# Moving the chain that makes dt ahead in four engines' orders, and one of its additions from GpSimd to VectorE

## The chip, the cores and the metric

The kernel runs on one core of a Trainium2 chip. The metric is the device time of one execution in microseconds, the median of several executions. Engine names are those of the profile: PE is TensorE, DVE is VectorE, ACT is ScalarE, POOL is GpSimd, and SP is the engine whose queue issues nearly all DMAs. A core's engines run their own instruction lists in order and meet only through semaphores.

## The reference

A decoder block over x of shape (4, 512, 512): first a Mamba layer with an MLP on the layer-normed input, then a quantized attention-like product, then a feed-forward layer with 4-bit weights. The change touches only the Mamba part, which is, cut to what matters:

```
zxbcdt = x @ in_proj_w.T                        # z, x, B, C and dt_in
dt  = softplus(dt_in @ dt_proj_w.T + dt_proj_b) # 1024 channels, 512 tokens
dA  = exp(dt[..., None] * A)                    # 16 states per channel
dBx = (dt * x) (x) B
h_i = dA_i * h_(i-1) + dBx_i                    # the recurrence over the tokens
y   = sum over the states of C_i * h_i, + D_skip * x
out = (y * silu(z)) @ out_proj_w.T
```

For large negative arguments the logarithm in softplus loses digits. The kernel computes softplus(v) = max(v, 0) + log(1 + e) + ((1 - (1 + e)) + e) with e = exp(-|v|); the last bracket is what 1 + e lost by rounding. The first half of the bracket, 1 - (1 + e), is made by ACT in two instructions into `sp_abs`; the addition of e is the one that the change moves.

## The kernel before, in words

The first stage, up to about 1034 us of 2797, is the scan. It runs over 32 steps (`g`): 4 batches times 8 tiles of 128 channels. Each step has 16 units (`c`), one for each state, each a tile of 128 partitions by 512 tokens. Per unit:

- PE spreads one row group of v = dt * x over the partitions (`spread_v`, from the tile `vpack`) and one of dt (`spread_dt`, from `dpack`), both with the selection matrix `sel` (both are L1806);
- ACT makes the decay exp(dt * A) in place in PSUM (`decay`, L896);
- DVE multiplies v by B (`make_drive`, L1392, tile `drive`) and runs the recurrence (`scan`, L1401, tile `state`). DVE's list is drive of the next unit, scan of this unit, and so on;
- POOL multiplies the state by C (`read_out`, L1233, tile `read`), and PE sums four of these at a time into y (`gather_four`, L1822, and L1820 for the skip term at the first four).

The scan of unit n waits for its decay; `spread_dt` of unit n+3 waits for the scan of unit n, as three PSUM banks are in turn. `read_out` uses a ring of 8 tiles, so its unit n waits until the gather of unit n-8 is done, and `state` is a ring of 6.

Beside this, step g makes what step g+1 and g+2 need, as lines spread over the units:

- in units 0 to 11 PE makes three tiles (jobs) of the input projection (L1757 to L1759, tiles `whi`, `wlo`), which ACT takes to SBUF (`take`, L830) and SP stores to DRAM (`spill`, L536) and later reads again. Step g with (g + 2) mod 8 = 7 has no jobs. The tiles of x and B of a new batch come in steps 6, 14 and 22, and each goes out in four scattered copies, `x_d<-ev` and `b_d<-ev`;
- the softplus for step g+2: PE makes the product (`dt_project`, unit 11), ACT then runs `soft_abs`, `soft_pos`, `soft_exp`, `soft_one` (two instructions) and `soft_log` at units 12 to 15;
- the rest of dt for step g+1: POOL runs `soft_rest` (the moved addition, tile `sp_rest`, L1182), `soft_sum` (L1188), `soft_dt` (L1197, tile `dt_t`) and `dt_x` (L1205, tile `v_t`) after the read_out of units 0, 1, 2, 3. ACT rounds dt and v to the PE's format (`dt_high` L872 at unit 6, `v_high` L876 at unit 8), POOL makes the remainders (`dt_low` L1210 at unit 7, `v_low` L1215 at unit 9), and SP copies all four, in halves, to `dpack` and `vpack` (`load_pack_dt`, `load_pack_v`, L554 to L558);
- a few things more on POOL: `normalise` in steps 2 and 4 (four each), `out_weights_low` in steps 29 and 30 (L1221, two each).

All orders are written out by hand in the loops below. SP's list in a step is: load of B, weights and spill for the first job, load of C, store of y, weights for the second, dt and v packs, spill of the second job, load of x for g+2, weights and spill of the third. SP waits in that order, so a wait holds up all behind it.

After the scan come the output projection, the two MLP-like layers and the attention-like part, with PE as the busy engine. The change does not touch them.

## Time and profile before

| | |
|---|---|
| median of 3 runs | 2795.44 us (2795.18 to 2797.02) |
| the profiled execution's own time | 2799.06 us |
| its span | 2797.3 us |
| PE, DVE, ACT, POOL busy over the span | 94%, 74%, 43%, 46% |
| from 54.8 us to 1034 us (the scan) | PE 839.0, DVE 924.4, ACT 559.1, POOL 908.3 us busy of 979.2; mean PE clock 0.89 |
| from 1034 us on | PE 1739.9, DVE 1131.4, ACT 599.4, POOL 358.1 us busy of 1763.3; mean PE clock 1.00 |
| chain that ended last, by engine | PE 66%, DVE 9%, issue 8%, POOL 8%, ACT 4%, DMA 3% |

The first scan starts at 54.76 us and the last at 1027.4 us. A row of the timeline gives start, length, engine, line and operation, and in brackets how long the engine sat idle just before and what it waited for. The length of a DVE, ACT or POOL instruction is longer than what it costs its engine, since the next one starts a little before it ends; the difference of two starts is the cost.

### The profile page before, as it was taken

The page shows a single profiled execution, that of the slowest core. Times are in us where ns is not written, and L with a number is a line of the kernel's source. Part 1 is how long each engine was busy: PE and PEld are TensorE (multiplying, and loading weights), DVE is VectorE, ACT ScalarE, POOL GpSimd, SP SyncE. Part 2 cuts the span into 40 slices and gives each one's busy share as a digit, 9 for nine tenths or more (in the row PEclk, how much of TensorE's full clock was granted, in tenths as well). Part 3 has the DMA queues.
Part 4 walks back from the last instruction along what each step waited for, and adds up shares of the span by engine and source line. Part 5 has one row for each costly group of instructions (what it writes and reads, how often), then busy time and mean ns, then how long its engine had stood idle before and what let it go on. Part 6 is the DMA issues. An engine that isn't in the chain of part 4 may idle for free.

```text
span 2797.3 us, 32656 instructions
## 1 busy us (share of the span) xinstructions
PE 2618.7 (94%) x11152; PEld 1877.7 (67%) x11160; DVE 2082.0 (74%) x2656; ACT 1191.1 (43%) x1786; POOL 1285.8 (46%) x868
## 2 busy tenths in 40 slices
PE   7888888898889879999999999999999999999999
PEld 4443444454345337888888778788878788888887
DVE  5999899999999976543376677777877865555553
ACT  5655555555555635422254543343333422222221
POOL 4899899899999961210001023123222422222220
PEclk9999899899899879999999999999999999999999
DMA  7754655555465437121111112112111121111111
GB/s 248 220 165 129 180 150 139 166 158 148 125 182 160 132 113 266 54 76 53 62 51 61 40 44 69 46 46 68 46 39 46 45 53 46 51 48 50 49 46 68
DMA packets 152311, 275.37 MB, mean 98 GB/s; under 512 B 27344, under 2 KB 27856, under 8 KB 151632
## 3 DMA queue, kind: packets, MB, share of 16 engines
q1 hardware_dynamic: 152144, 273.27, 32.7%
q8 instruction: 89, 1.46, 0.2%
q14 instruction: 78, 0.64, 0.1%
HBM read 178.01 MB, written 61.34 MB: 86 GB/s over the span
## 4 chain that ended last, share of the span: by engine, by line
PE 66%; DVE 9%; issue 8%; POOL 8%; ACT 4%; DMA 3%; SPq 1%; POOLq 0%; DVEq 0%; ACTq 0%
PE ps L1757 19%; PE ps L1759 19%; PE ps L1758 19%; DVE state L1401 4%; POOL read L1233 4%; PE ps L1806 3%; PE ps L1822 3%; ACT ps L896 1%; DMA vpack<-vl 1%; DMA b_d<-ev 1%; PE ps L1966 1%; POOL dt_t L1197 1%; POOL sp_rest L1182 1%; PE ps L1940 1%; DMA uraw<-y_d 1%
## 5 line engine op out<-in xcount | busy, mean ns | idle before, releaser
L1233 POOL TENSOR_TENSOR read<-state,c_t 128x512 f32<-128x512 f32 x512 | 662.9, 1316 | 74.4 <-DVE state L1401 35.8
L1401 DVE TENSOR_TENSOR_SCAN state<-ps,drive 128x512 f32<-128x512 f32 x512 | 622.5, 1216 | 4.2 <-ACT ps L896 1.7
L1295 POOL TENSOR_TENSOR wdeq<-packed,scales 128x1024 f32<-128x1024 f16 x96 | 256.2, 2668 | 800.7 <-DVE packed L1530 800.7
L1757 PE MATMUL ps<-xh,ghi 128*128 128x512 f32 x1536 | 607.3, 395 | 0.0
L1759 PE MATMUL ps<-xh,glo 128*128 128x512 f32 x1536 | 598.0, 389 | 0.0
L1758 PE MATMUL ps<-xl,ghi 128*128 128x512 f32 x1536 | 597.8, 389 | 0.0
L896 ACT ACTIVATE ps<-ps,a_exp 128x512 f32<-128x512 f32 x512 | 337.2, 661 | 385.4 <-PE ps L1806 383.9
L1392 DVE TENSOR_TENSOR drive<-ps,b_t 128x512 f32<-128x512 f32 x512 | 344.2, 672 | 53.6 <-PE ps L1806 49.5
L1697 DVE TENSOR_TENSOR act_o<-act_o,ps 128x512 f32<-128x512 f32 x192 | 131.8, 686 | 284.6 <-PE ps L1759 283.2
L1153 ACT ACTIVATE ahi<-act_o 128x512 fp32r<-128x512 f32 x192 | 121.6, 633 | 520.6 <-DVE act_o L1697 520.6
L1757 PEld LDWEIGHTS ps<-xh,ghi 128*128 128x128 f32 x1536 | 288.4, 188 | 62.6 <-issue 3.1
L1758 PEld LDWEIGHTS ps<-xl,ghi 128*128 128x128 f32 x1536 | 288.5, 188 | 61.7 <-issue 3.1
L1759 PEld LDWEIGHTS ps<-xh,glo 128*128 128x128 f32 x1536 | 288.3, 188 | 60.2
L1806 PE MATMUL ps<-dpack,sel 128*128 128x512 f32 x512 | 244.0, 477 | 86.6 <-DVE state L1401 85.6
L1757 PE MATMUL ps<-ahi,ghi 128*128 128x512 f32 x768 | 304.4, 396 | 2.0 <-DVE alo L1704 2.0
L1759 PE MATMUL ps<-ahi,glo 128*128 128x512 f32 x768 | 299.6, 390 | 0.0
L1758 PE MATMUL ps<-alo,ghi 128*128 128x512 f32 x768 | 299.5, 390 | 0.0
L1806 PE MATMUL ps<-vpack,sel 128*128 128x512 f32 x512 | 243.5, 476 | 44.5 <-DMA vpack<-vl 33.0
L1683 DVE TENSOR_TENSOR res<-res,ps 128x512 f32<-128x512 f32 x192 | 131.0, 686 | 171.3 <-PE ps L1759 171.1
L1806 PEld LDWEIGHTS ps<-vpack,sel 128*128 128x128 f32 x512 | 102.6, 201 | 230.1 <-DVE drive L1392 96.5
L1806 PEld LDWEIGHTS ps<-dpack,sel 128*128 128x128 f32 x512 | 104.6, 204 | 180.7 <-DVE state L1401 170.9
L1019 ACT ACTIVATE ghi<-wdeq 128x1024 fp32r<-128x1024 f32 x96 | 101.1, 1053 | 269.3 <-POOL wdeq L1295 244.8
(197 smaller groups left out, 3842.0 us busy)
## 6 DMA issues: line engine op xcount, KB each, us to landing
whi<-w_d SPq DMA_DIRECT2D x63, 256.0 KB, 4.9
wlo<-w_d SPq DMA_DIRECT2D x63, 256.0 KB, 5.5
b_d<-ev SPq DMA_DIRECT2D x32, 256.0 KB
dpack<-dh SPq DMA_DIRECT2D x64, 128.0 KB, 4.4
dpack<-dl SPq DMA_DIRECT2D x64, 128.0 KB, 2.3
b_t<-b_d SPq DMA_DIRECT2D x32, 256.0 KB, 5.4
vpack<-vh SPq DMA_DIRECT2D x64, 128.0 KB, 2.3
vpack<-vl SPq DMA_DIRECT2D x64, 128.0 KB, 2.4
```

Of the source, the lines that this page charges most:

```text
L896: act.activation(ps[:, decay_bank(n), :], ps[:, decay_bank(n), :], ACT.Exp, scale=a_exp[:, col:col + 1]).then_inc(decay_ready, 1)
L1153: act.activation(ahi[n // 2][:, cols(n % 2)], act_o[n % 2][:, :], ACT.Copy)\
L1233: pool.tensor_tensor(read[:, n % RRING, :], state[:, n % SRING, :], c_t[:, g % 2, :], ALU.mult).then_inc(read_ready, 1)
L1295: pool.tensor_tensor(wdeq[:, :].rearrange("p (h n) -> p h n", h=2), codes, scale, ALU.mult).then_inc(deq, 1)
L1392: dve.tensor_tensor(drive[:, n % DRING, :], ps[:, 2 + n % 2, :], b_t[:, g % 2, :], ALU.mult).then_inc(drive_ready, 1)
L1401: dve.tensor_tensor_scan(state[:, n % SRING, :], ps[:, decay_bank(n), :], drive[:, n % DRING, :], 0.0, ALU.mult, ALU.add)\
L1683: dve.tensor_tensor(res[:, f, cols(b)], res[:, f, cols(b)], ps[:, free_bank(24 * E + 16 + k), :], ALU.add).then_inc(added, 1)
L1697: dve.tensor_tensor(act_o[n % 2][:, :], act_o[n % 2][:, :], ps[:, free_bank(24 * E + 2 * n + 1), :], ALU.mult)\
L1757: pe.matmul(out_, w_h, x_h, start=(start and k == 0), stop=False)
L1758: pe.matmul(out_, w_h, x_l, start=False, stop=False)
L1759: last = pe.matmul(out_, w_l, x_h, start=False, stop=(stop and k == n - 1))
L1806: pe.matmul(ps[:, bank, :], sel[:, 4 * (j % 2) + m, :], pack[j // 2][:, :], start=True, stop=True).then_inc(done, 1)
```

## The change

Five edits:

1. `soft_rest` is run by DVE, no longer by POOL: for q = 0 before the loop, for q = 1 after the first scan, and for q = g + 2 after the scan of unit 14 of each step g up to 29.
2. POOL runs `soft_sum` for step g+2 after the read_out of unit 15 of step g, and then in step g + 1 `soft_dt` at unit 0, `dt_x` at 1, `dt_low` at 3, `v_low` at 5 (they were at 2, 3, 7, 9).
3. ACT runs `dt_high` at unit 2 and `v_high` at unit 4 (they were at 6 and 8).
4. ACT runs `soft_abs` at unit 11, `soft_pos` and `soft_exp` at 12, `soft_one` at 13 and `soft_log` at 14.
5. SP issues the two pack loads before the weights of the second job.

All computed values stay the same, and so does the number of instructions.

The diff:

```
--- before.py
+++ after.py
@@ -667,11 +667,11 @@
                     load_c(g + 1)
                 if g >= 1:
                     store_y(g - 1)
-                if jobs:
-                    weights_after(first + 1)
                 if 0 <= g + 1 < STEPS:
                     load_pack_dt(g + 1)
                     load_pack_v(g + 1)
+                if jobs:
+                    weights_after(first + 1)
                 if jobs:
                     spill(first + 1)
                 if g + 2 < STEPS:
@@ -964,19 +964,19 @@
                     if jobs and c % 4 == 2 and c > 4:
                         take(first + c // 4 - 1)
                     if 0 <= g + 1 < STEPS:
-                        if c == 6:
+                        if c == 2:
                             dt_high(g + 1)
-                        if c == 8:
+                        if c == 4:
                             v_high(g + 1)
                     if nb < B:
+                        if c == 11:
+                            soft_abs(g + 2)
                         if c == 12:
-                            soft_abs(g + 2)
+                            soft_pos(g + 2)
+                            soft_exp(g + 2)
                         if c == 13:
-                            soft_pos(g + 2)
+                            soft_one(g + 2)
                         if c == 14:
-                            soft_exp(g + 2)
-                        if c == 15:
-                            soft_one(g + 2)
                             soft_log(g + 2)
             def silu_z(m):
                 b, c = divmod(m, OCH)
@@ -1175,13 +1175,6 @@
                 pool.wait_ge(ln_r1, b + 1)
                 pool.tensor_tensor(hat(b)[:, f, :], xlr[b][:, f, :], r1, ALU.mult).then_inc(ln_hat, 1)
 
-            def soft_rest(q):
-                pool.wait_ge(sp_one_ready, 2 * q + 2)
-                if q:
-                    pool.wait_ge(sp_sum_ready, q)
-                pool.tensor_tensor(sp_rest[:, :], sp_abs[:, :], sp_exp[:, :], ALU.add)\
-                    .then_inc(sp_rest_ready, 1)
-
             def soft_sum(q):
                 pool.wait_ge(sp_log_ready, q + 1)
                 pool.wait_ge(sp_rest_ready, q + 1)
@@ -1235,7 +1228,6 @@
 
             for f in range(FT):
                 normalise(0, f)
-            soft_rest(0)
             soft_sum(0)
             soft_dt(0)
             dt_x(0)
@@ -1250,19 +1242,20 @@
                         normalise(1 + g // 2, c // 4)
                     if g in (STEPS - 3, STEPS - 2) and c in (12, 14):
                         out_weights_low(2 * (g - STEPS + 3) + (c - 12) // 2)
+                    if g == 0 and c == 0:
+                        soft_sum(1)
                     if g + 1 < STEPS:
                         if c == 0:
-                            soft_rest(g + 1)
+                            soft_dt(g + 1)
                         if c == 1:
-                            soft_sum(g + 1)
-                        if c == 2:
-                            soft_dt(g + 1)
+                            dt_x(g + 1)
                         if c == 3:
-                            dt_x(g + 1)
-                        if c == 7:
                             dt_low(g + 1)
-                        if c == 9:
+                        if c == 5:
                             v_low(g + 1)
+                    if g + 2 < STEPS:
+                        if c == 15:
+                            soft_sum(g + 2)
             phase_end(pool, 1)
  
 
@@ -1381,6 +1374,13 @@
                 dve.wait_ge(dthi_ready, nb + 1)
                 dve.tensor_tensor(dtlo[:, :], ps[:, 5 + (IN_TILES * nb) % 2, :],
                                   dthi[:, :].bitcast(F32), ALU.subtract).then_inc(dtlo_ready, 1)
+
+            def soft_rest(q):
+                dve.wait_ge(sp_one_ready, 2 * q + 2)
+                if q:
+                    dve.wait_ge(sp_sum_ready, q)
+                dve.tensor_tensor(sp_rest[:, :], sp_abs[:, :], sp_exp[:, :], ALU.add)\
+                   .then_inc(sp_rest_ready, 1)
 
             def make_drive(g, c):
                 n = NST * g + c
@@ -1421,6 +1421,7 @@
             dve.wait_ge(a_ready, 1)
             dve.tensor_scalar(a_exp[:, :], a_exp[:, :], -1.0, None, ALU.mult).then_inc(a_ready, 1)
             centre(1)
+            soft_rest(0)
             w_low(3)
             centre(2)
             w_low(4)
@@ -1436,6 +1437,10 @@
                     elif g + 1 < STEPS:
                         make_drive(g + 1, 0)
                     scan(g, c)
+                    if g == 0 and c == 0:
+                        soft_rest(1)
+                    if nb < B and c == 14:
+                        soft_rest(g + 2)
                     if g == 0 and c == 1:
                         w_low(5)
                     for b in (1, 2, 3):
```

On POOL, around the border of two steps (any from 6 on). Before, three more instructions stand between the last `read` of a step and `dt_t`, each with a `read` between:

```order
L1233 TENSOR_TENSOR read<-state,c_t 128x512 x7
L1182 TENSOR_TENSOR sp_rest<-sp_abs,sp_exp 128x512
L1233 TENSOR_TENSOR read<-state,c_t 128x512
L1188 TENSOR_TENSOR sp_log<-sp_log,sp_rest 128x512
L1233 TENSOR_TENSOR read<-state,c_t 128x512
L1197 TENSOR_TENSOR dt_t<-sp_log,sp_pos 128x512
```

and in the changed kernel, at the same border (line numbers are 7 lower here):

```order
L1226 TENSOR_TENSOR read<-state,c_t 128x512 x10
L1181 TENSOR_TENSOR sp_log<-sp_log,sp_rest 128x512
L1226 TENSOR_TENSOR read<-state,c_t 128x512
L1190 TENSOR_TENSOR dt_t<-sp_log,sp_pos 128x512
L1226 TENSOR_TENSOR read<-state,c_t 128x512
L1198 TENSOR_TENSOR v_t<-dt_t,x_t 128x512
L1226 TENSOR_TENSOR read<-state,c_t 128x512 x2
L1203 TENSOR_TENSOR dl<-dt_t,dh 128x512
```

The sum now comes ahead of the step's first `read`, and `dt_t` stands behind the first one where it stood behind the third.

On ACT, at the start of a step; `ps<-ps,a_exp` is the decay of one unit, and the row `skip_w` stands behind the decay of unit 1. Before:

```order
L883 ACTIVATE skip_w<-ident,d_skip 128x128
L896 ACTIVATE ps<-ps,a_exp 128x512 x5
L890 ACTIVATE y_t<-ps 128x512
L830 ACTIVATE ev<-ps 128x512
L872 ACTIVATE dh<-dt_t 128x512
```

and now:

```order
L883 ACTIVATE skip_w<-ident,d_skip 128x128
L896 ACTIVATE ps<-ps,a_exp 128x512
L872 ACTIVATE dh<-dt_t 128x512
L896 ACTIVATE ps<-ps,a_exp 128x512 x2
L876 ACTIVATE vh<-v_t 128x512
```

Where five decays stood ahead of the rounding of dt (`dh`), one does; the decay of unit 3 and all later ones now stand behind it.

On SP in step 6, the step in which x and B of the next batch are made. Before:

```order
L593 DMA y_d<-y_t 128x512
L517 DMA whi_80<-w_d 128x512
L518 DMA wlo_83<-w_d 128x512
L554 DMA dpack_102<-dh 64x512
L555 DMA dpack_103<-dh 64x512
L557 DMA dpack_102<-dl 64x512
L558 DMA dpack_103<-dl 64x512
L554 DMA vpack_106<-vh 64x512
L555 DMA vpack_107<-vh 64x512
L557 DMA vpack_106<-vl 64x512
L558 DMA vpack_107<-vl 64x512
L536 DMA x_d<-ev 128x512 x4
```

and now:

```order
L593 DMA y_d<-y_t 128x512
L554 DMA dpack_102<-dh 64x512
L555 DMA dpack_103<-dh 64x512
L557 DMA dpack_102<-dl 64x512
L558 DMA dpack_103<-dl 64x512
L554 DMA vpack_106<-vh 64x512
L555 DMA vpack_107<-vh 64x512
L557 DMA vpack_106<-vl 64x512
L558 DMA vpack_107<-vl 64x512
L517 DMA whi_80<-w_d 128x512
L518 DMA wlo_83<-w_d 128x512
L536 DMA x_d<-ev 128x512 x4
```

The packs stand ahead of the second job's weights; the spill of x stays behind both.

## Rows read from the trace of the kernel before

**Rows 1.** The decays, on the page: line, engine, output, input, count | busy, mean ns | idle before.
```profile
L896 ACT ACTIVATE ps<-ps,a_exp 128x512 f32<-128x512 f32 x512 | 337.2, 661 | 385.4 <-PE ps L1806 383.9
```
**Rows 2.** Timeline of DVE at the border of steps 6 and 7.
```profile
280.60 1.22 DVE L1401 TENSOR_TENSOR_SCAN state<-ps,drive 128x512 f32<-128x512 f32 x1
...
286.57 0.69 DVE L1392 TENSOR_TENSOR drive<-ps,b_t 128x512 f32<-128x512 f32 x1 [1.33 <-PE ps L1806]
...
290.60 1.22 DVE L1401 TENSOR_TENSOR_SCAN state<-ps,drive 128x512 f32<-128x512 f32 x1
```
**Rows 3.** Timeline of PE at the same border: the gather behind unit 0.
```profile
283.87 1.93 PE L1822 MATMUL ps<-read,gather 128*32 128x512 f32 x8
```
**Rows 4.** Timeline of DVE: the same place at the borders 5/6 and 27/28.
```profile
257.10 0.69 DVE L1392 TENSOR_TENSOR drive<-ps,b_t 128x512 f32<-128x512 f32 x1 [0.81 <-PE ps L1806]
...
914.81 0.69 DVE L1392 TENSOR_TENSOR drive<-ps,b_t 128x512 f32<-128x512 f32 x1 [0.66 <-PE ps L1806]
```
**Rows 5.** Timeline of POOL at the border of steps 6 and 7.
```profile
283.60 1.27 POOL L1233 TENSOR_TENSOR read<-state,c_t 128x512 f32<-128x512 f32 x1 [0.43 <-DVE state L1401]
286.01 1.28 POOL L1233 TENSOR_TENSOR read<-state,c_t 128x512 f32<-128x512 f32 x1 [1.13 <-PE ps L1822]
287.25 1.30 POOL L1182 TENSOR_TENSOR sp_rest<-sp_abs,sp_exp 128x512 f32<-128x512 f32 x1
```
**Rows 6.** Timeline of POOL, then ACT, then DVE in step 30.
```profile
980.69 1.28 POOL L1197 TENSOR_TENSOR dt_t<-sp_log,sp_pos 128x512 f32<-128x512 f32 x1
...
982.01 0.63 ACT L872 ACTIVATE dh<-dt_t 128x512 fp32r<-128x512 f32 x1 [3.88 <-POOL dt_t L1197]
...
983.27 1.22 DVE L1401 TENSOR_TENSOR_SCAN state<-ps,drive 128x512 f32<-128x512 f32 x1 [1.20 <-issue]
```
**Rows 7.** Timeline of DVE, the drive of unit 10 in steps 7 and 23; then PE.
```profile
304.85 0.69 DVE L1392 TENSOR_TENSOR drive<-ps,b_t 128x512 f32<-128x512 f32 x1 [4.47 <-PE ps L1806]
...
785.45 0.69 DVE L1392 TENSOR_TENSOR drive<-ps,b_t 128x512 f32<-128x512 f32 x1 [3.90 <-PE ps L1806]
...
299.94 0.50 PE L1757 MATMUL ps<-xh,whi 128*128 128x512 f32 x1 [2.42 <-DMA wlo<-w_d]
```
**Rows 8.** The chain that ended last, 280 to 310 us: start, us, what.
```profile
287.09 7.33 DMA b_d<-ev
...
295.28 4.62 DMA wlo<-w_d
```
**Rows 9.** Timeline of ACT (the second job's take), then SP, in step 6.
```profile
272.25 0.59 ACT L830 ACTIVATE ev<-ps 128x512 f32<-128x512 f32 x1
...
277.37 0.60 SPq L558 DMA_DIRECT2D vpack<-vl  x1
278.01 2.08 SPq L536 DMA_DIRECT2D x_d<-ev  x4
...
285.11 3.20 SPq L536 DMA_DIRECT2D b_d<-ev  x4
```
**Rows 10.** Timeline of DVE, then POOL: additions that read two SBUF tiles.
```profile
120.62 0.67 DVE L1376 TENSOR_TENSOR wlo<-wraw,whi 128x512 fp32r<-128x512 f32 x1
...
129.03 1.11 DVE L1365 SCALAR_TENSOR_TENSOR xlr<-xlr,rms,dwraw 128x512 f32<-128x512 f32 x1
...
120.78 1.63 POOL L1233 TENSOR_TENSOR read<-state,c_t 128x512 f32<-128x512 f32 x1 [0.43 <-DVE state L1401]
```
**Rows 11.** Timeline of POOL, then DVE, in step 0.
```profile
60.43 1.28 POOL L1233 TENSOR_TENSOR read<-state,c_t 128x512 f32<-128x512 f32 x1 [12.15 <-DMA c_t<-c_d]
...
62.93 1.22 DVE L1401 TENSOR_TENSOR_SCAN state<-ps,drive 128x512 f32<-128x512 f32 x1 [0.21 <-ACT ps L896]
```
**Rows 12.** Timeline of DVE, then POOL, at the border of steps 4 and 5.
```profile
223.10 0.69 DVE L1392 TENSOR_TENSOR drive<-ps,b_t 128x512 f32<-128x512 f32 x1 [2.04 <-issue]
...
230.55 1.22 DVE L1401 TENSOR_TENSOR_SCAN state<-ps,drive 128x512 f32<-128x512 f32 x1
...
229.05 1.27 POOL L1233 TENSOR_TENSOR read<-state,c_t 128x512 f32<-128x512 f32 x1
```

More of the change, by code:

```diff
@@ L669, in _ @@
                     store_y(g - 1)
-                if jobs:
-                    weights_after(first + 1)
                 if 0 <= g + 1 < STEPS:
@@ L674, in _ @@
                     load_pack_v(g + 1)
+                if jobs:
+                    weights_after(first + 1)
                 if jobs:
@@ L966, in _ @@
                     if 0 <= g + 1 < STEPS:
-                        if c == 6:
+                        if c == 2:
                             dt_high(g + 1)
-                        if c == 8:
+                        if c == 4:
                             v_high(g + 1)
                     if nb < B:
+                        if c == 11:
+                            soft_abs(g + 2)
                         if c == 12:
-                            soft_abs(g + 2)
+                            soft_pos(g + 2)
+                            soft_exp(g + 2)
                         if c == 13:
-                            soft_pos(g + 2)
+                            soft_one(g + 2)
                         if c == 14:
-                            soft_exp(g + 2)
-                        if c == 15:
-                            soft_one(g + 2)
                             soft_log(g + 2)
@@ L1176, in normalise @@
                 pool.tensor_tensor(hat(b)[:, f, :], xlr[b][:, f, :], r1, ALU.mult).then_inc(ln_hat, 1)
-            def soft_rest(q):
-                pool.wait_ge(sp_one_ready, 2 * q + 2)
-                if q:
-                    pool.wait_ge(sp_sum_ready, q)
-                pool.tensor_tensor(sp_rest[:, :], sp_abs[:, :], sp_exp[:, :], ALU.add)\
-                    .then_inc(sp_rest_ready, 1)
             def soft_sum(q):
@@ L1252, in _ @@
                         out_weights_low(2 * (g - STEPS + 3) + (c - 12) // 2)
+                    if g == 0 and c == 0:
+                        soft_sum(1)
                     if g + 1 < STEPS:
                         if c == 0:
-                            soft_rest(g + 1)
+                            soft_dt(g + 1)
                         if c == 1:
-                            soft_sum(g + 1)
-                        if c == 2:
-                            soft_dt(g + 1)
+                            dt_x(g + 1)
                         if c == 3:
-                            dt_x(g + 1)
-                        if c == 7:
                             dt_low(g + 1)
-                        if c == 9:
+                        if c == 5:
                             v_low(g + 1)
+                    if g + 2 < STEPS:
+                        if c == 15:
+                            soft_sum(g + 2)
             phase_end(pool, 1)
@@ L1383, in dt_split, with soft_rest @@
                                   dthi[:, :].bitcast(F32), ALU.subtract).then_inc(dtlo_ready, 1)
+            def soft_rest(q):
+                dve.wait_ge(sp_one_ready, 2 * q + 2)
+                if q:
+                    dve.wait_ge(sp_sum_ready, q)
+                dve.tensor_tensor(sp_rest[:, :], sp_abs[:, :], sp_exp[:, :], ALU.add)\
+                   .then_inc(sp_rest_ready, 1)
             def make_drive(g, c):
@@ L1423, in _ @@
             centre(1)
+            soft_rest(0)
             w_low(3)
@@ L1438, in _ @@
                     scan(g, c)
+                    if g == 0 and c == 0:
+                        soft_rest(1)
+                    if nb < B and c == 14:
+                        soft_rest(g + 2)
                     if g == 0 and c == 1:
```

1 line of the change is left out of this document (removed).

## The prediction

> **What bounds the kernel now.** I read the page's slices first: up to about 1034 us (the scan) DVE is the busiest engine, and after it PE works almost without a break. The change touches only the scan, so what it is worth there arrives at the end as it stands. Next come the idle times of DVE inside the scan, since DVE's list (drive, scan, drive, scan) is what a step lasts. Without waits a unit costs it 1.71 us: from the drive of unit 2 to the scan of unit 3 it is 4.03 us, two periods and one drive of 0.61 [rows 2]. Sixteen make 27.4 us, and steps without other work or waits do come to 28. What DVE waits for falls in three kinds:
>
> - At the border of two steps, before the drive of unit 2. The scan of unit 14 starts at 280.60 and ends at 281.82. PE's work behind it (spread, three matmuls of a job, a gather of 1.93 us at the 1.2 GHz level) lets the drive of unit 2 start only at 286.57 [rows 2, 3]. Idle 1.33. Over the 24 borders from 5/6 to 28/29 there are 20 such waits, between 0.17 and 1.33 us; nine are of 1.33, four borders have none, and the other eleven sum to 6.4 us ([rows 2, 4] show one of the nine, and the first and the last of the eleven).
> - In steps 7, 15 and 23, before the drive of unit 10: three waits, the first 4.47 and the last 3.90 us [rows 7], the one between 4.17. The chain of waits names the cause: the scattered stores of B, then the load of `wlo` for the step's third job, which SP may issue only behind B's load [rows 8].
> - Single ones: 2.04 at the end of step 4 [rows 12], 1.20 in step 30 [rows 6].
>
> ACT is no bound in the mean: it sat idle 385 us before its decays [rows 1]. But it stands between POOL's dt and DVE's scan, and this is where I expect the price.
>
> **The chain of dt, the new floor of a step's start.** Step 30 shows what a late `dt_t` does today. It ends at 980.69 + 1.28 = 981.97. ACT, which had waited 3.88 us, rounds it, makes the next decay, and DVE's scan starts at 983.27: 1.30 us after the end of `dt_t`, with 1.20 idle [rows 6]. So no scan behind `dh` in ACT's list can start earlier than 1.30 us after the end of `dt_t`. Today the first one behind it is the scan of unit 7. In the changed kernel it is that of unit 3, while `dt_t` itself waits for `read` of unit 15, the sum, and `read` of unit 0.
>
> I put the changed order on the border 6/7. POOL has caught up there: `read` of unit 15 starts 0.07 us behind its scan [rows 5], and with one addition less per step it will have again. DVE: the addition goes in behind the scan of unit 14, at 0.58 us (below), so the scan of unit 15 starts at 280.60 + 1.71 + 0.58 = 282.89 and ends at 284.11. POOL: `read` 15 at 284.18; two POOL instructions lie 1.25 apart (286.01 to 287.25 [rows 5]), so sum 285.43, `read` 0 at 286.68 (the gather that it waited for at 286.01 is over), `dt_t` from 287.93 to 289.21. Scan of unit 3 not before 290.51. Today it starts at 290.60 [rows 2]: no loss at a border with 1.33. From the start of the scan of unit 14 the floor is thus 9.91 us. A border without a wait needs 5 x 1.71 = 8.56, so it loses 1.35; a border with an idle time I loses 1.35 less I and 0.09 (an idle of 1.33 moves the later starts by 1.42). The added addition is inside this number, not beside it. Sum for 24 borders: 24 x 1.35 = 32.4, less 9 x 1.35 = 12.2, less 6.4 + 11 x 0.09 = 7.4: **+12.9 us**.
>
> The early steps and step 30, each by the same rule:
> - Step 0: `read` of unit 0 cannot start before 60.43 (C's load) [rows 11]. Sum and dt end 3 x 1.25 + 0.03 later, 64.2; the scan of unit 3, today at 62.93 [rows 11], then starts at 65.5: +2.6.
> - Border 0/1 has no wait: +1.35. Border 1/2 waits on PE behind the next scan, so the addition pushes all: +0.6. Border 2/3 had a wait of 1.0: 0. Border 3/4: +1.35.
> - Border 4/5: POOL is behind, because of `normalise`. `read` 0 of step 5 starts at 229.05 [rows 12] and one POOL instruction less stands ahead of it: 227.8. `dt_t` ends 2.5 later, the scan of unit 3 starts at 231.6 instead of 230.55 [rows 12]; 0.3 of a later wait goes: +0.75, with the 2.04 us (a late `vpack`) already in it.
> - Step 30: `dt_t` comes four or so POOL instructions sooner, at 977.6 instead of 981.97 (two reads, two additions moved, one added, less what was idle). The scan of unit 3 then starts at 978.95 and that of unit 7 at 985.8, against 983.27 [rows 6]: +2.5, of which I give back 0.2 for a late `vpack`. **Sum +8.9 us.**
>
> **The addition on DVE.** No row shows this addition there. The nearest are additions of the same shape that read two SBUF tiles [rows 10]: 0.67 long, 0.58 to the next start, where DVE starts first and POOL's `read` beside it takes 1.63 instead of 1.28; 1.11 long, about 1.04, where POOL is at work. Behind the scan of unit 14 POOL starts only when that scan has ended, as at 120.78 [rows 10], so I take 0.58. Bounds: below nothing is excluded, since DVE must run it; 0 where a wait hides it; at the top 1.04, which would put 0.46 on each of the 15 borders and 0.36 on the nine: +10 us.
> The Trainium skill has a rule on this ("SBUF — State Buffer", the section on engine ports): a VectorE instruction with two SBUF inputs and a GpSimd one that reads SBUF take the shared port in turn, whoever starts first holding it to its end. The trace agrees in direction (0.67 beside 1.63, 1.11 in the other order). By the rule a read of 1.28 begun first could cost up to its whole length; the sum goes by the rows.
>
> **What SP's order gives.** In step 6 ACT has taken the second job (x) at 272.25 + 0.59 = 272.84, but SP is still at the packs: the last half of `vl` is issued at 277.37 and the four stores of x at 278.01 [rows 9]. Behind them stand x's load, the weights and the stores of B at 285.11 [rows 9], then B's load, and 4.62 us after 295.28 `wlo` lands, at 299.90 [rows 8]. In the new order `v_low` is over near 270.2 (`read` 0 of step 6 at 257.7, nine POOL instructions of 1.25 behind it, 1.3 for the last), the packs and the weights are issued by 272.4, and x goes out at 272.9: 5.1 us earlier. B goes out at about 280.5, as its take moves behind two more ACT instructions: 4.6 earlier, and `wlo` lands near 295.3. PE had waited for it 2.42 us before 299.94 [rows 7], from about 297.5, so the wait is gone with 2 us to spare. Without it, unit 10's drive is on time, as in the steps next to these. Gain 4.47 + 4.17 + 3.90: **-12.5 us**.
> The other moves hide: the weights behind the packs are needed only at the next step's start, and ACT's softplus, closer packed in units 11 to 14, keeps by my count about 0.6 us before each decay. Were that margin gone, 0.5 us a step or 15 us would be the price; I keep part of it in the range. The earlier packs alone give nothing else: PE's spread of unit 0 was not what DVE waited for, except at the border 4/5.
>
> **Sum.** 12.9 + 8.9 - 12.5 = +9.3 us. The profiled execution took 2799.06 us by its own time, so the changed one should take about 2808.4. The runs shown have a median 3.6 us lower, 2795.44: **2804.7 us**.
>
> **The rivals.**
> 1. *POOL's chain is in time, so no floor* (faster). If `dt_t` ended 1.3 us earlier than I count, only the addition would remain, partly hidden in the waits: 4 x 0.58 + 0.3 + 2 x 0.3 = 3.2 at the 24 borders, about +2 on the first ones and step 30 less the 2.04, and the gain of 12.5 in full: -8 to -9, **2787**. For it: POOL loses 32 additions of 1.29 and the late `dh` waits of today vanish. Against: it needs three POOL instructions and two roundings to fit in five DVE units, and rows 5 and 6 say that they do not.
> 2. *Half of the floor* (within 0.2%). Idle times at the borders that come from PE's clock may move, and POOL's steps of 1.25 may be shorter: half of 12.9 + 8.9, less 12.5: -1.6, **2794 to 2799**.
> 3. *The addition meets POOL's read* (slower still): 1.04 each, + 10: **2815**. It decides if POOL is behind by unit 14.
> 4. *SP's relief fails*, for instance if B's scattered stores last longer beside other DMAs: + 12.5: **2817**.
> PE's clock would be a fifth: at the border it is at 1.2 GHz [rows 3]. The Trainium skill ("TensorE: Matmul & The Clock Gate", Part 1) lets the clock fall after idle time, and the earlier packs take idle time away. If the clock stayed at 2.4 GHz the wait of 1.33 would go, but the floor of 9.91 stays in its place: no gain.
>
> **Chances.** Forecast 0.48, its own range 2799 to 2811, with a tenth of it under the bound of 0.2% (2801; 0.2% is about what a measurement of this kernel can tell from no change). Rival 1 0.18, rival 2 0.18, rival 3 0.12, rival 4 0.04. Slower by over 0.2%: 0.43 + 0.12 + 0.04 = 0.59; within: 0.18 + 0.05 = 0.23; faster: 0.18. The range for 8 in 10 reaches from rival 1 to just past rival 3: 2787 to 2816.
>
> **What the changed profile would show.** Right: ACT waits before `dh` for `dt_t` at nearly every step (some 2 us or more each, where today six short ones stand), and DVE idles before the scan of unit 3, released by the decay; steps last 28.7 to 29 us with little spread; 32 additions of 0.67 on DVE; the waits of 4 us in steps 7, 15 and 23 gone, x's stores issued about 5 us earlier in steps 6, 14 and 22. Wrong: no idle before the scan of unit 3 (rival 1), `sp_rest` of 1 us on DVE (rival 3), a PE wait for `wlo` in step 7 (rival 4).

## The result, and the profile after

The changed kernel took 2813.41 us (median of 4 runs, 2810.45 to 2814.54), the kernel before, run beside it, 2796.23 us: ratio 1.0059 [1.0041, 1.0076], some 17 us slower. The direction and the mechanism were forecast; the number, 2804.7, was 8.7 us too low. It lies in the range (2787 to 2816), 2.6 us under its top, but outside the forecast's own (2799 to 2811).

The profiled execution of the changed kernel was the shortest of its four: own time 2810.45, span 2808.7. Its page, the rows that answer to [rows 1] and those of the waiting engines (line numbers as in the changed kernel, where PE's spreads are L1811):

```profile
L1401 DVE TENSOR_TENSOR_SCAN state<-ps,drive 128x512 f32<-128x512 f32 x512 | 618.7, 1209 | 20.1 <-DVE drive L1392 8.8
L896 ACT ACTIVATE ps<-ps,a_exp 128x512 f32<-128x512 f32 x512 | 331.4, 658 | 286.5 <-PE ps L1811 285.7
L1392 DVE TENSOR_TENSOR drive<-ps,b_t 128x512 f32<-128x512 f32 x512 | 340.8, 666 | 24.7 <-PE ps L1811 23.5
```

Before, DVE idled 53.6 us ahead of its drives (three stalls of 12.5 in sum among them) and 4.2 ahead of its scans. Now it is 24.7 and 20.1: the stalls are gone, and a new wait stands before the scan. ACT's 385.4 before the decays has become 286.5, and this row of the view by lines says where two thirds of it went:

```profile
L872 ACT ACTIVATE dh<-dt_t 128x512 fp32r<-128x512 f32 x32 | 20.2, 632 | 76.6 <-POOL dt_t L1190 76.6
```

Before it was 10.4 us. (The rounding of v, `vh`, took on another 18.9: 24.7 for 5.8.) ACT now stands waiting at the rounding of dt in nearly every step, with the decay of unit 3 and all later ones behind it.

The border of steps 6 and 7, which [rows 2, 5] show of before (timeline of DVE, then POOL, then ACT):

```profile
290.79 1.21 DVE L1401 TENSOR_TENSOR_SCAN state<-ps,drive 128x512 f32<-128x512 f32 x1
291.92 0.66 DVE L1382 TENSOR_TENSOR sp_rest<-sp_abs,sp_exp 128x512 f32<-128x512 f32 x1
...
296.24 0.69 DVE L1392 TENSOR_TENSOR drive<-ps,b_t 128x512 f32<-128x512 f32 x1 [0.22 <-PE ps L1811]
...
299.69 0.66 DVE L1392 TENSOR_TENSOR drive<-ps,b_t 128x512 f32<-128x512 f32 x1
300.73 1.22 DVE L1401 TENSOR_TENSOR_SCAN state<-ps,drive 128x512 f32<-128x512 f32 x1 [0.37 <-DVE drive L1392]
...
292.07 1.65 POOL L1226 TENSOR_TENSOR read<-state,c_t 128x512 f32<-128x512 f32 x1 [0.43 <-DVE state L1401]
294.39 1.28 POOL L1226 TENSOR_TENSOR read<-state,c_t 128x512 f32<-128x512 f32 x1 [0.67 <-DVE state L1401]
295.62 1.30 POOL L1181 TENSOR_TENSOR sp_log<-sp_log,sp_rest 128x512 f32<-128x512 f32 x1
296.87 1.31 POOL L1226 TENSOR_TENSOR read<-state,c_t 128x512 f32<-128x512 f32 x1
298.12 1.31 POOL L1190 TENSOR_TENSOR dt_t<-sp_log,sp_pos 128x512 f32<-128x512 f32 x1
...
299.46 0.63 ACT L872 ACTIVATE dh<-dt_t 128x512 fp32r<-128x512 f32 x1 [2.33 <-POOL dt_t L1190]
300.00 1.22 ACT L896 ACTIVATE ps<-ps,a_exp 128x512 f32<-128x512 f32 x2
```

From the scan of unit 14 (290.79) to that of unit 3 (300.73) it is 9.94 us; the prediction had 9.91. The chain is read downwards: read 15 at 294.39, three more POOL instructions 1.25 apart, ACT's rounding at 299.46, the scan 1.27 later. DVE's wait names its own drive as the releaser, but that drive ended at 299.69 + 0.66 = 300.35, before the scan; the one that came last is the decay that ACT could make only behind `dh` (the first of the two at 300.00). At nine of the 24 borders from 5/6 to 28/29 DVE waits 0.73 us for PE before the drive of unit 2 instead, and the length comes out about the same (10.00 us at the border 7/8).

The stall of [rows 7] in step 7 is gone: SP comes to x's stores sooner in step 6 ([rows 9] show the same rows of before). Whether SP's own new order or the earlier packs did this, experiments h and o below tell.

```profile
280.27 0.60 SPq L558 DMA_DIRECT2D vpack<-vl  x1
280.96 0.54 SPq L517 DMA_DIRECT2D whi<-w_d  x1
281.55 0.46 SPq L518 DMA_DIRECT2D wlo<-w_d  x1
283.05 1.94 SPq L536 DMA_DIRECT2D x_d<-ev  x4
```

Counted from the step's first scan (265.21), x's stores now go out at 17.84 us; before it was 278.01 - 255.07 = 22.94. That is the 5.1 us of the prediction. B's stores, behind them, go out 4.5 us earlier (25.53 for 30.04 us into the step; the prediction had 4.6).

And the border of steps 4 and 5 ([rows 12]), where the prediction was furthest off (POOL, then DVE):

```profile
227.17 3.75 POOL L1226 TENSOR_TENSOR read<-state,c_t 128x512 f32<-128x512 f32 x3
233.28 1.27 POOL L1226 TENSOR_TENSOR read<-state,c_t 128x512 f32<-128x512 f32 x1 [2.36 <-DVE state L1401]
234.50 1.28 POOL L1176 TENSOR_TENSOR xhr<-xlr,row_r 128x512 f32<-128x512 f32 x1
...
228.97 2.50 DVE L1382 TENSOR_TENSOR sp_rest<-sp_abs,sp_exp 128x512 f32<-128x512 f32 x1
...
240.77 1.22 DVE L1401 TENSOR_TENSOR_SCAN state<-ps,drive 128x512 f32<-128x512 f32 x1 [1.85 <-issue]
```

POOL is behind there and runs three reads without a gap. The addition starts in the second of them and ends only 0.55 us behind the third, 2.50 us long. POOL then waits 2.36 us for the scans that the addition delayed, so the whole chain to `dt_t` starts later. DVE's own wait before the scan of unit 3, 1.85 us, is not the long addition's: in h below the addition took 0.83 us here and that wait was 1.88. A `normalise` (the row at 234.50) stands in POOL's chain at this border and makes the floor longer.

**Where the time is.** The table cuts the profiled executions at the first scan of a step. "Changed" is the mean of three: the one above, a repeat, and one with SP's order as before (h below); their spans are 2808.7, 2816.2 and 2814.9 us.

| stretch, us | before | changed: mean (lowest, highest) | difference | predicted |
|---|---|---|---|---|
| start to the first scan | 54.8 | 55.9 (55.4, 56.5) | +1.1 | 0 |
| steps 0 to 5 | 200.3 | 209.6 (208.8, 210.2) | +9.3 | +6.7 |
| the 20 steps from 6 to 28 without 7, 15, 23 | 587.5 | 598.2 (596.2, 600.7) | +10.7 | +11.0 |
| steps 7, 15, 23 | 98.8 | 87.2 (87.1, 87.3) | -11.6 | -12.0 |
| steps 29, 30 | 59.0 | 62.8 (62.5, 63.1) | +3.8 | +3.7 |
| from the first scan of step 31 on | 1796.9 | 1799.6 (1796.9, 1802.3) | +2.7 | 0 |
| sum | 2797.3 | 2813.3 | +16.0 | +9.3 |

(The predicted column is the prediction's own terms, each border counted in the step that pays for it.) The first pair of profiles alone would have shown +11.4.

### The profile page after: what moved, and what is told of

The parts are those of the page before. It is cut to its first block, busy times and chain, and to the rows that moved or that the text cites. A ratio compares the mean times of both kernels' runs of the same rounds, so it can differ in the third digit from the quotient of the medians.

```text
span 2808.7 us, 32664 instructions
## 1 busy us (share of the span) xinstructions
PE 2642.7 (94%) x11160; PEld 1882.4 (67%) x11160; DVE 2103.0 (75%) x2688; ACT 1178.3 (42%) x1786; POOL 1258.0 (45%) x836
## 4 chain that ended last, share of the span: by engine, by line
PE 62%; DVE 11%; issue 10%; POOL 9%; ACT 5%; DMA 1%; SPq 1%; POOLq 0%; DVEq 0%; ACTq 0%
PE ps L1762 18%; PE ps L1763 18%; PE ps L1764 18%; POOL read L1226 6%; DVE state L1401 6%; ACT ps L896 2%; PE ps L1811 2%; PE ps L1827 1%; POOL dt_t L1190 1%; DVE drive L1392 1%; PE ps L1825 1%; PE ps L1971 1%; DMA uraw<-y_d 1%; PE ps L1945 1%; POOL v_t L1198 1%
## 5 line engine op out<-in xcount | busy, mean ns | idle before, releaser
L1226 POOL TENSOR_TENSOR read<-state,c_t 128x512 f32<-128x512 f32 x512 | 676.0, 1338 | 111.3 <-DVE state L1401 94.8
L1401 DVE TENSOR_TENSOR_SCAN state<-ps,drive 128x512 f32<-128x512 f32 x512 | 618.7, 1209 | 20.1 <-DVE drive L1392 8.8
L896 ACT ACTIVATE ps<-ps,a_exp 128x512 f32<-128x512 f32 x512 | 331.4, 658 | 286.5 <-PE ps L1811 285.7
L1392 DVE TENSOR_TENSOR drive<-ps,b_t 128x512 f32<-128x512 f32 x512 | 340.8, 666 | 24.7 <-PE ps L1811 23.5
L1811 PE MATMUL ps<-dpack,sel 128*128 128x512 f32 x512 | 252.0, 492 | 107.8 <-DVE state L1401 106.9
L1811 PE MATMUL ps<-vpack,sel 128*128 128x512 f32 x512 | 249.0, 487 | 20.4 <-DVE drive L1392 13.0
L1811 PEld LDWEIGHTS ps<-dpack,sel 128*128 128x128 f32 x512 | 105.6, 206 | 217.9 <-DVE state L1401 210.5
L1811 PEld LDWEIGHTS ps<-vpack,sel 128*128 128x128 f32 x512 | 104.5, 204 | 212.1 <-DVE drive L1392 100.3
```

Of the source, the lines that this page charges most:

```text
L896: act.activation(ps[:, decay_bank(n), :], ps[:, decay_bank(n), :], ACT.Exp, scale=a_exp[:, col:col + 1]).then_inc(decay_ready, 1)
L1226: pool.tensor_tensor(read[:, n % RRING, :], state[:, n % SRING, :], c_t[:, g % 2, :], ALU.mult).then_inc(read_ready, 1)
L1392: dve.tensor_tensor(drive[:, n % DRING, :], ps[:, 2 + n % 2, :], b_t[:, g % 2, :], ALU.mult).then_inc(drive_ready, 1)
L1401: dve.tensor_tensor_scan(state[:, n % SRING, :], ps[:, decay_bank(n), :], drive[:, n % DRING, :], 0.0, ALU.mult, ALU.add)\
L1811: pe.matmul(ps[:, bank, :], sel[:, 4 * (j % 2) + m, :], pack[j // 2][:, :], start=True, stop=True).then_inc(done, 1)
```

## The experiments

Theory: the cost is a floor under each step's start (POOL's chain from read 15 to `dt_t`, then ACT, then the first scan behind `dh`); the gain is the three stalls at unit 10, gone because v's packs leave SP's queue earlier. Main rival: the cost is the 32 additions on DVE. Kernels of one set ran on the same chip with runs of the kernel before between them (medians 2798.06, 2800.25 and 2796.75 us in the three sets), so the ratios are what to compare.

**a_after**: the changed kernel again.

> The changed kernel again, unchanged, so that the others of this set have it beside them. Theory (the floor at the scan of unit 3, less what the three stalls at unit 10 gave back): again 0.4 to 0.7% over the kernel before, 2808 to 2815 us; in the profile, 9.9 us from the start of the scan of unit 14 to that of unit 3 at the borders from 5/6 on. Open is why the profiled pair stands 11.4 us apart and the medians 17: if that was one draw of the profile, the new profile shows lengths of steps that sum to some 16 us more than before; if it lies outside the span, the profile is again near 2809.

Measured 2816.05 us, 1.0061 [1.0048, 1.0073]. The profiled execution is 7.5 us longer than the first of the same code: 2.8 us behind the scan, the rest in the scan, most of it in steps 13, 18 and 21. It stands 18.9 us over the profile of before where the first stood 11.4 over it, so the first was a short draw. From the scan of unit 14 to that of unit 3 it is 9.87 to 10.15 us at 18 of the 24 borders; at the other six (10.9 to 11.6) other work stands in DVE's list. In step 21 (no jobs for PE) the difference is one wait. Two of PE's rows, then DVE's, of the repeat:

```profile
732.05 1.91 PE L1825 MATMUL ps<-x_t,skip_w 128*128 128x512 f32 x2
733.89 1.94 PE L1827 MATMUL ps<-read,gather 128*32 128x512 f32 x8
...
736.59 0.69 DVE L1392 TENSOR_TENSOR drive<-ps,b_t 128x512 f32<-128x512 f32 x1 [1.76 <-PE ps L1811]
```

and of the first profile, where DVE did not wait at this unit:

```profile
728.84 1.02 PE L1825 MATMUL ps<-x_t,skip_w 128*128 128x512 f32 x2
729.79 1.07 PE L1827 MATMUL ps<-read,gather 128*32 128x512 f32 x8
```

The same matmuls, at a granted clock of 0.50 (1.2 GHz) in the one and 1.00 (2.4 GHz) in the other by the windows of those 4 us. The wait before the drive of unit 10 lies between nothing and 1.76 us in steps 13 and 21 over these profiles, and varies in steps 5 and 29 too. The Trainium skill ("TensorE: Matmul & The Clock Gate", Part 1) has the clock follow how busy TensorE has been; the trace agrees so far that these are the steps in which TensorE has no jobs, but no run here shows why one execution falls and the other does not.

**b_round4**: dt rounded two units later; the additions stay.

```
-    if c == 2: dt_high      if c == 4: v_high      # ACT
+    if c == 4: dt_high      if c == 6: v_high
-    if c == 3: dt_low       if c == 5: v_low       # POOL
+    if c == 5: dt_low       if c == 7: v_low
```

> The changed kernel with ACT rounding dt at unit 4 (v at 6) and GpSimd's remainders at units 5 and 7; all else as changed. Theory (what costs is that dt_t is late for the scan behind dh): the first scan behind the rounding is that of unit 5, 3.4 us later in DVE's list, so the floor of 9.91 us no longer binds; ACT's wait before dh falls under 0.6 us. Only what is left of 32 additions remains (about +4 to +6) less the 12.5 of the three stalls: 2787 to 2791 us, below the kernel before. Rival (the 32 additions on DVE are the price, 32 x 0.58 = 18.6 us, wherever ACT rounds): no change against the changed kernel, 2808 to 2815. Second rival (the later packs bring the stalls at unit 10 in steps 7, 15 and 23 back): +12 on the first, 2800.

Measured 2795.72 us, 0.9987 [0.9978, 0.9996]: 20 us under the changed kernel with all additions still on DVE. ACT's waits before `dh` fell from 76.6 to 8.1 us, DVE's before its scans from 20.1 to 2.8. The main rival fell, and so did the second: steps 7, 15 and 23 took 85.8 us, without the stalls. It was not the 2787 to 2791 forecast: its 20 steady steps (third row of the table) are 594.1 us, 4 under the changed kernel's mean and 6.6 over before.

**c_rest_pool**: the addition back on POOL, ACT as changed.

```
-    if nb < B and c == 14: soft_rest(g + 2)        # DVE, behind the scan
+    if c == 14: soft_rest(g + 2)                   # POOL, behind the read
```

> The changed kernel with the addition given back to GpSimd, at the place that VectorE had it (behind the read of unit 14). Theory (the chain on GpSimd from the read of unit 15 to dt_t is the floor): GpSimd then has read 14, addition, read 15, sum, read 0, dt_t, one more instruction of 1.25 us; VectorE has 0.58 us less; from the scan of unit 14 the scan of unit 3 comes 1.22 + 5 x 1.25 + 1.28 + 1.30 = 10.1 us after, where it is 9.9 now. So it gains nothing: within 3 us of the changed kernel or 2 to 5 us above it, less some 2 us at the border 4/5 where VectorE's addition took 2.50: 2808 to 2818. Rival (the additions on VectorE are the price): 18.6 us less, 2792 to 2796.

Measured 2816.95 us, 1.0070 [1.0057, 1.0084]: giving DVE its 32 additions back gains nothing. Steady steps (9, 15 and 17, for instance) went from 29.0 or 29.1 to 29.2 us, the 10.1 - 9.9 us of the floor. The theory held, in the time and in the step.

**d_spill_first**: the kernel before, the second job's stores ahead of the packs in every step.

```
+                if jobs: spill(first + 1)
                 load_pack_dt(g + 1); load_pack_v(g + 1)
-                if jobs: spill(first + 1)
```

> The kernel before, but with SP issuing the stores of the second job ahead of the dt and v packs; nothing else moved. Theory (the stalls of 4.47, 4.17 and 3.90 us at unit 10 of steps 7, 15 and 23 come from x's and B's stores standing behind late packs in SP's list): the three waits go, 12.5 us less: 2783 to 2785; if the packs, now behind the stores, come late at these three borders, up to 1 us of each is given back. Rival (the wait there is B's scattered stores and the load behind them, however early they are issued, or the give-back came from the earlier packs): the waits stay, 2795 to 2797.

Measured 2807.39 us, 1.0030 [1.0019, 1.0041]: slower, against both. The three stalls went (steps 7, 15, 23: 87.0 us for 98.8), but steps 8, 16 and 24 now end in a wait as long. SP, then PE, at the end of step 8:

```profile
330.97 3.35 SPq L536 DMA_DIRECT2D b_d<-ev  x4
334.43 1.17 SPq L554 DMA_DIRECT2D dpack<-dh  x1
...
341.06 0.60 SPq L558 DMA_DIRECT2D vpack<-vl  x1
...
343.43 0.80 PE L1806 MATMUL ps<-vpack,sel 128*128 128x512 f32 x1 [6.38 <-DMA vpack<-vl]
```

The packs stood behind stores that waited for their own take, and PE waited 6.38 us for the last. The edit was too coarse, not the mechanism wrong; experiment i below has it in three steps alone.

**e_dve_add_alone**: the kernel before, with the addition on DVE behind the scan of unit 0.

> The kernel before with only the addition moved to VectorE, behind the scan of unit 0 of the step in which GpSimd made it; nothing else moved. Theory (an addition costs 0.58 to 0.66 where no wait hides it and GpSimd leaves the port free, and only a few meet GpSimd's reads standing back to back): it stands before the drive of unit 2, so nine waits of 1.33 hide it, eleven hide about half, and some twelve borders pay 0.6: +8 to +12 with one or two long ones as the 3.74 us that the last set showed at the border 4/5; 2805 to 2810 us beside 2798 for the kernel before. Rival (it costs its length at every border): +19 to +21, 2817 or more. Second rival (the work that GpSimd no longer does pays for it): within 3 us of before.

Measured 2803.81 us, 1.0020 [1.0007, 1.0034], about +5.6 with an interval of +2 to +10: less than the theory's +8 to +12 and more than the second rival's 3, so it lies between them. Where a wait of 1.33 stood it shrank to 0.75 and the step kept its length (step 8: 29.09 for 29.14); in all the 20 steps took 592.2 us for 587.5. Three additions are long: 1.54 us in step 3, 2.26 in step 30, and the longest of all at the border 4/5 (DVE, then the POOL instructions beside it):

```profile
225.61 4.59 DVE L1379 TENSOR_TENSOR sp_rest<-sp_abs,sp_exp 128x512 f32<-128x512 f32 x1
...
222.25 4.96 POOL L1226 TENSOR_TENSOR read<-state,c_t 128x512 f32<-128x512 f32 x4
227.17 1.25 POOL L1176 TENSOR_TENSOR xhr<-xlr,row_r 128x512 f32<-128x512 f32 x1
228.39 1.25 POOL L1226 TENSOR_TENSOR read<-state,c_t 128x512 f32<-128x512 f32 x1
```

It started inside the reads and ended at 230.20, 0.56 us behind the end of the last POOL instruction of an unbroken row (229.64).

**f_round4_pool**: b and c together: no floor, and no addition on DVE.

> The changed kernel with dt rounded at unit 4 and with the addition given back to GpSimd behind the read of unit 14. Theory: the first edit takes the floor away (the set before: 20 us), and then the additions on VectorE are a cost that is seen: some 15 borders without a wait at 0.58 = 9, and the 3.74 us at the border 4/5; so 10 to 13 us under the version that has only the first edit (2795.7): 2783 to 2786, the best of all so far. Rival (the additions are hidden in VectorE's waits for TensorE, which come back when they are gone): 2793 to 2797, as without it.

Measured 2793.69 us, 0.9982 [0.9971, 0.9993]. The theory missed here by 8 to 11 us and the rival was right. Where b waits 0.73 us at a border, f waits 1.33; at the border 7/8:

```profile
315.26 0.69 DVE L1396 TENSOR_TENSOR drive<-ps,b_t 128x512 f32<-128x512 f32 x1 [1.33 <-PE ps L1810]
```

Step 8 took 29.09 in f and 29.18 in b. Without the floor PE sets most borders, and an addition of 0.6 only fills part of its wait. What f gains on DVE is in step 4 (29.5 for 32.7); it gives 1.6 back in step 5 and 3.8 in step 30, where DVE waits again before the first scan behind `dh` (0.83 and 1.56 us before that of unit 5).

**g_round3**: dt rounded one unit later than changed.

> The changed kernel with ACT rounding dt at unit 3 (v at 5) and GpSimd's remainders at 4 and 6: one unit later than changed, one earlier than in the version that was 20 us faster. Theory (a floor of 9.91 us from the scan of unit 14 to the first scan behind dh): that scan is now that of unit 4, which without waits comes 6 x 1.71 + 0.58 = 10.84 after the scan of unit 14, so the floor has 0.9 us to spare and one unit is enough: 2793 to 2799 us, the same as with two units. Rival (every unit that dt's chain is moved ahead costs its share, for instance by what ACT and TensorE then have in a row): half way, 2804 to 2808.

Measured 2799.39 us, 1.0001 [0.9990, 1.0013]. Just past the upper end of the theory and far from the half-way rival. Its 20 steady steps, 592.8 us, are no longer than b's 594.1; it stands above b in steps 0 to 5 (+3.4) and 29, 30 (+3.6), where `dt_t` is later than at a normal border and one unit is not enough.

**h_sp_as_before**: the changed kernel with edit 5 undone.

> The changed kernel with edit 5 undone: SP issues the weights of the second job ahead of the packs again. Theory (the stalls in steps 7, 15 and 23 went because v's remainder is ready 8 us earlier, not because SP issues the packs ahead of the weights): no change, within 3 us of the changed kernel, 2812 to 2818. Rival (edit 5 is what made room): the three stalls come back, +12: 2825 to 2830.

Measured 2815.11 us, 1.0056 [1.0037, 1.0076]: no change. SP's edit is worth nothing by itself.

**i_spill_three_steps**: d's edit in steps 6, 14 and 22 only.

> The kernel before, with SP issuing the second job's stores ahead of the packs in steps 6, 14 and 22 only (in the version that did it in every step, the waits in steps 7, 15 and 23 went, but the steps 8, 16 and 24 ended with waits of 4.4 to 4.8 us, since the packs then stood behind B's stores). Theory: the three waits of 4.5, 4.2 and 3.9 us go and nothing comes in their place, 10 to 12.5 us less than the kernel before: ratio 0.9955 to 0.9965, about 2787 beside 2799. Rival (the time comes back in the waits for TensorE at the borders or at unit 10 of the other steps): less than 4 us, ratio above 0.9985.

Measured 2791.67 us, 0.9976 [0.9965, 0.9988], the lowest ratio of all, though its interval overlaps those of b, f and l; between the two forecasts. Steps 7, 15 and 23 lost 11.1 us. Steps 6, 14 and 22 grew by 3.8 (the packs are late there: 0.72, 0.63 and 1.42 us before the drive of the next step's unit 0), and the other 17 of the 20 by 2.4, half of it in step 13, where the wait before unit 10 was 1.76 us for 0.59.

**l_one_on_pool**: b with the one addition of step 4 on POOL.

> The changed kernel with dt rounded at unit 4, and one single addition, that of step 4, given back to GpSimd; the other 31 stay on VectorE. Theory: the one addition that met three of GpSimd's reads standing back to back was 3.74 us long instead of 0.66, so step 4 takes 29.5 us instead of 32.65; half of it may come back in step 5: 1.5 to 3 us under the version with all additions on VectorE, whose ratio to before was 0.9987, so 0.9976 to 0.9982. Rival (the addition waited for nothing that its place decides): 0.9987 again.

Measured 2793.36 us, 0.9986 [0.9976, 0.9996]: no gain over b that can be told. Step 4 did fall, from 32.65 to 28.95 us, but step 5 grew from 28.34 to 31.13, with waits before the scan of unit 5 (0.81, the first scan behind `dh`) and the drive of unit 10 (1.96) that b did not have. So the 3.74 us of b's long addition are seen by DVE, and without it nearly the same time goes in other waits.

**n_dt_before_read**: the changed kernel, `dt_t` ahead of the read of unit 0; ACT untouched.

```
+                    if c == 0 and 1 <= g < STEPS - 1: soft_dt(g + 1)
                     read_out(g, c)
-                        if c == 0: soft_dt(g + 1)
```

> The changed kernel with dt_t made ahead of the read of unit 0 in steps 1 to 30, so 1.25 us sooner; ACT still rounds it at unit 2. Theory (the floor is GpSimd's chain read 15, sum, read 0, dt_t): the floor from the scan of unit 14 to that of unit 3 falls from 9.9 to 8.7 us, under the 9.1 that VectorE needs with its addition; the waits before the scan of unit 3 go at the middle borders and lose 1.25 us in steps 5 and 30: 8 to 11 us less than the changed kernel's 2815, so 2804 to 2807. Rival (the price is ACT's order itself, a rounding in front of the decays): no change, 2813 or more. Second rival (the later read of unit 0 holds up the gather and the ring of states): slower than changed.

Measured 2802.55 us, 1.0021 [1.0011, 1.0031], by the ratios 10 to 11 us under the changed kernel (1.0056 to 1.0061), where 8 to 11 were forecast. The same border as above (POOL, then DVE):

```profile
294.35 1.27 POOL L1181 TENSOR_TENSOR sp_log<-sp_log,sp_rest 128x512 f32<-128x512 f32 x1
295.69 1.27 POOL L1190 TENSOR_TENSOR dt_t<-sp_log,sp_pos 128x512 f32<-128x512 f32 x1
...
295.49 0.69 DVE L1394 TENSOR_TENSOR drive<-ps,b_t 128x512 f32<-128x512 f32 x1 [0.73 <-PE ps L1813]
...
299.56 1.21 DVE L1403 TENSOR_TENSOR_SCAN state<-ps,drive 128x512 f32<-128x512 f32 x1
```

The scan of unit 3 no longer waits; the wait is PE's, before the drive of unit 2, as in b. In step 30, where POOL is later still, the wait before the scan of unit 3 fell from 3.46 to 2.35, and in step 5 from 1.86 to 0.74.

**o_v_late**: the changed kernel with v's two steps back at units 8 and 9.

> The changed kernel with v's rounding and remainder back at units 8 and 9 (as before), dt's left at units 2 and 3. Theory (the three stalls went because v's packs were over 5 us earlier, so that SP came to x's stores in time): they come back, 12 us more than changed: 2824 to 2829, ratio about 1.010. Rival (it is dt's pack, or the weights issued behind the packs): no change, ratio 1.006.

Measured 2829.61 us, 1.0112 [1.0094, 1.0129]. The stalls are back, of 5.47, 3.98 and 4.16 us. Timeline of SP, then DVE:

```profile
289.67 0.60 SPq L558 DMA_DIRECT2D vpack<-vl  x1
...
291.44 2.47 SPq L536 DMA_DIRECT2D x_d<-ev  x4
...
319.03 0.69 DVE L1392 TENSOR_TENSOR drive<-ps,b_t 128x512 f32<-128x512 f32 x1 [5.47 <-PE ps L1811]
```

x's stores went out at 291.44 - 268.37 = 23.07 us into the step, as before (22.94). Together with h: what removed the stalls was the earlier `v_low`, not SP's own edit.

## Why the prediction was right, and where it was too low

- **The floor.** Shown from three sides. The length between the two scans was 9.94 for 9.91; moving the consumer (b, g) or the producer (n) by one place or two takes it away at the ordinary borders; lengthening the chain (c) adds some 0.1 to 0.2 to a step. From the scan of unit 14 to that of unit 3 the 24 borders sum to 232.8 us before and to 246.0, 247.2 and 246.0 in the three profiles of the changed kernel: +13.6 in the mean for +12.9 predicted. The other part of the 20 steady steps, from the scan of unit 3 to that of unit 14, is as long as it was: 390.6 us before and 390.0, 390.3 and 390.2 after, if the waits before unit 10 of steps 13 and 21 are left out. So edit 4, ACT's closer softplus, which has no run of its own, shows no price.

  One thing the term hides: the floor takes the place of other time. The versions without it did not come back to before's 587.5 us in the 20 steps. They took 592.0 to 594.1 (b, e, f, g, i, l and n; d, with its late packs, 604.5), so taking the floor away gives back only 4 to 6 of the +10.7. Of the rest, one part is the addition where no wait hides it: the borders in front of steps 13 and 21 took 9.17 and 9.16 us in b for 8.56 in both before. But f has no addition on DVE and stands 5.0 over before all the same. Of that 3.2 are waits for PE before the drive of unit 2 (18.3 us in the 20 steps for 15.1). Why they are longer is not shown, nor whether the one profile of the kernel before was short in this stretch; if it was, the close match of +10.7 and +11.0 is partly luck.
- **The addition at 0.58.** Right for 29 of the 31 in the loop (0.65 to 0.67 long); the last, in step 29, took 0.89, and it was wrong at the border 4/5, where the prediction had looked for a late `vpack` and POOL's place in its list but not for DVE's addition in the middle of POOL's reads. That is the step that failed: "+0.75" there. From the scan of unit 14 of step 4 to that of unit 3 of step 5 it was 10.72 us before, 12.93 and 14.20 in the two profiles of the changed kernel (additions of 2.50 and 3.75), and 11.28 in h, where the addition took 0.83: +0.56 for +0.75. Steps 4 and 5 together grew by 2.2 + 1.9 = 4.1 us in the first profile, for 2.1 predicted (1.35 and 0.75), and by 2.5 in h. Rival 3 named exactly this condition ("if POOL is behind by unit 14"), with 1.04 as the top of the price; at this border it was far more.
- **Steps 29 and 30.** +3.8 for +3.7. The wait before the scan of unit 3 in step 30 was there, 3.45 us. That the sum agrees so well is partly luck: step 29 grew by 2.2 and step 30 by 1.6 in the mean, where the prediction had 1.35 and 2.3, and the waits before unit 10 of these steps vary by half a microsecond to one.
- **The three stalls.** -11.6 for -12.0, with x's stores 5.1 us earlier as worked out, and shown by o and h to hang on v's rounding and remainder, not on edit 5. Rival 4 fell.
- **Rivals 1 and 2.** Fell for the changed kernel. What rival 1 described ("no floor") is version b; the prediction gave it 2787, it took 2796. By the ratio it is 3.6 us under before where rival 1 had 8 to 9: too hopeful by some 5 us, about what the versions without the floor take over before in the steady steps.
- **Not in any term:** +1.1 before the first scan and +2.7 behind the scan. Versions whose code there is that of the kernel before (d, i) also started 1.1 and 1.7 us later than its profile, and the end took 1794.7 to 1802.2 us over the 14 profiles with no order in it (b 1802.2, f 1797.7, n 1794.7). I read both as scatter of single executions. One profiled pair was a poor measure of a 0.6% effect: +11.4 in the first pair, +16 for the mean of three, +17 and +18 by the medians.

## What to carry to other kernels

Before moving work earlier in an in-order engine's list, add up the producer's chain to it and compare that with the time at which the first thing behind it is needed; moving the consumer further ahead than its producer can follow costs time, and here one unit later for the consumer, or one instruction sooner for the producer, took most of the loss away. A stall that comes from a queue is cured by whatever lets the queue go on (here v's remainder, or a reordering in three steps of 32), and a reordering made in every step moves the stall to another. When a wait for the second-slowest engine stands at a border, work taken off the first one is only turned into that wait.

## What the runs showed of the hardware that was not expected

- An addition of 0.66 us on VectorE that reads two SBUF tiles can lose to several GpSimd instructions in a row. At the border 4/5, where GpSimd ran without a gap, it took 2.50, 3.72 to 3.75 (five profiles) and 4.59 us, and ended about 0.55 us behind the last instruction of the unbroken row. But this is no rule for every such row. Elsewhere the addition came in when the one GpSimd instruction that was running ended: 0.83 us in h, 0.84 in b (step 5), 1.54 and 2.26 in e, and 0.89 or 0.90 in step 29 of every version that has it there. Timeline of DVE, then POOL, of the changed kernel in step 29:

```profile
975.90 0.89 DVE L1382 TENSOR_TENSOR sp_rest<-sp_abs,sp_exp 128x512 f32<-128x512 f32 x1
...
973.88 2.36 POOL L1214 TENSOR_TENSOR owlo<-owraw,owhi 128x1024 fp32r<-128x1024 f32 x1
976.20 2.95 POOL L1226 TENSOR_TENSOR read<-state,c_t 128x512 f32<-128x512 f32 x2
```

  It ended 0.55 us behind `owlo` (976.24), with two reads following without a gap, the first of them lengthened. What decides between the two cases is not shown. The Trainium skill ("SBUF — State Buffer", section "SBUF: two separate sides") has whoever starts first hold the shared port to the end of its instruction and the other blocked. The trace agrees that it blocks; how many instructions it can lose to, the page does not say: at the border 4/5 the 1.8 to 3.9 us over the normal length are up to three of GpSimd's. VectorE's drives and scans, which take one operand from PSUM, kept their 0.66 and 1.21 beside the same reads.
- The other way round the loss is small: a GpSimd read that starts 0.15 us behind such an addition takes 1.65 us instead of 1.28, and one that follows where the addition comes in between takes 1.72.
- TensorE's clock in the scan differs between executions of one program at the same place (1.91 and 1.02 us for the same two matmuls, granted clock 0.50 and 1.00), and with it the wait of VectorE behind (1.76 us or none). The waits before unit 10 of steps 5, 13, 21, 29, 30 and 31, where TensorE has no jobs, sum to 6.3 us in one profile of the changed kernel and to 8.2 in the next.
